# Gated cross-attention and quantised FFN on one core: input weights quantised in the drain, the first norm applied after the query projection, one-hots of batches 1 to 3 on GpSimd

## Chip, cores and metric

One core of one Trainium2 chip runs the whole layer. The metric is device time in microseconds of one execution. Engine names: PE (TensorE, with PEld for its weight loads), DVE (VectorE), ACT (ScalarE), POOL (GpSimd), SP (the queue that issues most loads).

## What is computed

x has 4 batches of 1024 rows of 256. Each row attends to 4 consecutive rows of a small context (77 rows), found by its segment number, with 16 heads of 16; then an FFN 256 to 1024 to 256 whose weights and activations are quantised.

```python
def reference(x, ctx_1024, itok_BxS_0_511, g_xattn, g_ffn, L0_xattn_Wq, L0_xattn_Wkv, L0_xattn_Wo, L0_ffn_W_in, L0_ffn_b_in, L0_ffn_W_out, L0_ffn_b_out):
    # _layernorm(x): (x - mean) / sqrt(var + 1e-5) over the last axis
    def _L0_xattn_ref(q, kv_src, seg_id, Wq, Wkv, Wo):      # 16 heads of 16, SCALE = 0.25
        qh = _split_heads(q @ Wq.T)
        k, v = jnp.split(kv_src @ Wkv.T, 2, axis=-1)
        kh, vh = _split_heads(k), _split_heads(v)
        gather = seg_id[:, :, None] - jnp.arange(4)
        neg_mask = gather < 0
        gc = jnp.clip(gather, 0, lkv - 1)
        k_sel, v_sel = kh[b_idx, :, gc], vh[b_idx, :, gc]
        scores = einsum('bhqd,bhqkd->bhqk', qh, k_sel) * SCALE
        probs = softmax(where(neg_mask, -inf, scores))
        return einsum('bhqk,bhqkd->bhqd', probs, v_sel).reshape(b, lq, 256) @ Wo.T
    def _L0_ffn_ref(x, W_in, b_in, W_out, b_out):
        # quantize_w8_per: round to 127 levels of the absolute maximum of a column (W_in) or a row (W_out)
        # quantize_a16: round to 32767 levels of the absolute maximum of the whole tensor
        hidden = gelu(quantize_a16(x) @ quantize_w8_per(W_in, 0) + b_in)
        return quantize_a16(hidden) @ quantize_w8_per(W_out, 1) + b_out
    x = x + tanh(g_xattn[0]) * _L0_xattn_ref(_layernorm(x), ctx_1024, itok_BxS_0_511, L0_xattn_Wq, L0_xattn_Wkv, L0_xattn_Wo)
    x = x + tanh(g_ffn[0]) * _L0_ffn_ref(_layernorm(x), L0_ffn_W_in, L0_ffn_b_in, L0_ffn_W_out, L0_ffn_b_out)
```

## The kernel before

The work is straight engine programs joined by semaphores. There are NT = 32 tiles of 128 rows, handled in NP = 16 pairs; TB = 8 tiles make a batch. The kernel has four parts.

**Setup.** Context and weights are transposed on PE. `project_kv(b)` makes K and V of a batch in PSUM, `kv_scales` and `kv_high`/`kv_low` split them into two f16 halves in `kvtab`. `clamp_seg(b)` (L903) clamps the segment numbers of a batch, broadcast over 80 partitions, and `make_onehot(b)` (L910) compares them with the partition number: four one-hot matrices of 80 x 1024, by which PE gathers K and V rows as matmuls. `neg` holds the mask of rows whose segment number is below the offset. The query weights are transposed into `wqT`.

**The attention steps.** `step(i)` exists on every engine and is a software pipeline over pairs: the first norm of pair i (`stats(0)`, `aggregate(0)`, `norm_bias`, `norm1`), transpose and query projection of pair i; products and scores of pair i-1 (`qk`, `qk_sum`, `mask`, `score_max`, `shift`); softmax and weighting of V of pair i-2 (`exp`, `exp_sum`, `probs`, `copy_v`, `weigh_v`); output projection and residual of pair i-3; second norm of pair i-4 (`stats(1)`, `aggregate(1)`, `norm2`); its transpose and maximum for pair i-5. Steps 1 to 5 and 16 to 20 are written out, 6 to 15 are a loop of two steps an iteration. Within a step DVE runs in the order: statistics, exp sum, aggregate (L796, it releases POOL), reciprocal, `probs` (L847), `qk` (L811), `norm_bias` (L803), sum (L817), `qk`, sum, `largest` (L860), `mask` (L823), `residual` (L854), `score_max`, `shift` (L832). POOL runs `inv_std` (L268, L270, the power -0.5) and then `weigh_v` for two tiles: L278 (products), L281 and L285 (sums). PE has one PSUM pair of banks for K (`ps_k`) and one for V (`ps_v`), so each gather waits until the tile before has been read.

**The weights of the FFN.** W_in is transposed into PSUM in two halves (`win_T`), scaled per row (`win_scales` on DVE), rounded to int16 and made f16 (`round_win` on ACT), transposed back (`win_back`) and kept as `win8`; this happens between steps 1 and 3. W_out is rounded on DVE in steps 19 and 20 (L989 to L1002), and its maximum over partitions is a GpSimd `partition_all_reduce` (L303).

**The FFN.** After step 20 (the drain) the maximum of the normed x over partitions (L307) gives the scale; stage B is `expand` on PE (L728), Gelu on ACT, `hidden_max` and `quantise_x` on DVE, 8 groups of 4 tiles; POOL adds the output bias to the residual (L313). After a last maximum (L316) stage C is `contract` (L757) with the rounding on ACT and DVE.

## Time and profile before

| | us |
|---|---|
| median of 3 runs | 381.46 (380.48 to 418.29) |
| the profiled execution, its own time | 379.69 |
| its span, first to last instruction | 377.9 |
| mean granted TensorE clock | 0.918 |
| DVE busy, share of the span | 313.8, 83% |
| PE busy, share of the span | 289.2, 77% |
| ACT busy, share of the span | 225.0, 60% |
| POOL busy, share of the span | 179.9, 48% |

The profiled execution lies 0.8 us below the fastest run. Its span leaves out 1.8 us that lie around it. Busy shares are means over parts with different limits: setup and first steps to about 77 us, attention steps to 220 us, the drain to 250.2 us, stage B to 308 us, stage C to 370 us.

### The profile page before, as it was taken

To read this page: it belongs to the slowest core of one execution; us is meant where nothing else is said; L and a number is where in the kernel's file an instruction comes from. 1 tells how busy PE (TensorE), PEld (TensorE's weight loads), DVE (VectorE), ACT (ScalarE), POOL (GpSimd) and SP (SyncE) were. 2 spreads that over 40 slices of the span, in tenths; PEclk is the share of its full clock that TensorE was granted. 3 is DMA by queue.
4 is the path that set the end of the run, shared out by engine and by line. 5 is a ranking of instruction groups with operands and counts; after the bars stand their busy time and mean duration, and the time that the engine had idled before them with its cause. 6 is when DMAs were issued, how large, how long until landed. Compare 5 with 4: busy or idle time off the path is not lost.

```text
span 377.9 us, 6301 instructions
## 1 busy us (share of the span) xinstructions
PE 289.2 (77%) x1801; PEld 209.9 (56%) x1801; DVE 313.8 (83%) x583; ACT 225.0 (60%) x343; POOL 179.9 (48%) x167
## 2 busy tenths in 40 slices
PE   0685766778887987889887755159999958999991
PEld 0452555556665866667666544014444427888881
DVE  0278779998999999999999963668999969999990
ACT  1145265526556456555555552319999969999981
POOL 0110076687887797877788892113324500110011
PEclk9998769969999899998999986559999998999997
DMA  7991000000000000000000000001121210345438
GB/s 254 283 393 36 3 0 0 3 0 0 3 1 0 0 0 0 0 2 0 0 0 0 0 0 0 1 3 56 78 88 56 99 69 0 57 62 91 69 56 113
DMA packets 7117, 17.71 MB, mean 47 GB/s; under 512 B 1334, under 2 KB 3838, under 8 KB 6590
## 3 DMA queue, kind: packets, MB, share of 16 engines
q1 hardware_dynamic: 4447, 12.57, 9.4%
q0 software_dynamic: 1296, 4.19, 7.4%
q10 hardware_dynamic: 1359, 0.76, 0.8%
q8 instruction: 8, 0.13, 0.1%
q14 instruction: 7, 0.06, 0.1%
HBM read 9.13 MB, written 8.39 MB: 46 GB/s over the span
## 4 chain that ended last, share of the span: by engine, by line
PE 43%; DVE 35%; issue 15%; POOL 3%; ACT 2%; DVEq 1%; POOLq 0%; ACTq 0%
PE bank L728 15%; PE bank L757 15%; DVE prod L811 9%; PE bank L608 6%; DVE s L817 5%; PE bank L588 3%; DVE bn L788 3%; DVE onehot L910 2%; DVE xres L854 2%; DVE nbias L803 1%; DVE mv L796 1%; PE bank L566 1%; POOL vsel L278 1%; DVE srec L841 1%; DVE s L823 1%
## 5 line engine op out<-in xcount | busy, mean ns | idle before, releaser
L588 PE MATMUL bank<-kvtab,onehot 80*128 (+1 forms) x512 | 71.4, 285 | 36.6 <-DVE prod L811 25.8
L588 PEld LDWEIGHTS bank<-kvtab,onehot 80*128 (+1 forms) x512 | 48.2, 101 | 56.9 <-issue 23.6
L278 POOL TENSOR_TENSOR vsel<-vsel,pr 128x1024 f32<-128x1024 f32 x32 | 61.7, 1930 | 0.0
L728 PE MATMUL bank<-xhi,win 128*128 128x512 f16 x128 | 49.7, 388 | 8.0 <-DVE xlo L1022 8.0
L487 ACT ACTIVATE hidden<-bank,bin__58,zscale 128x512 f32 x64 | 49.8, 778 | 8.0 <-PE bank L728 2.9
L728 PE MATMUL bank<-xlo,win 128*128 128x512 f16 x128 | 49.6, 387 | 0.0
L1074 DVE SCALAR_TENSOR_TENSOR hlo<-hq,rel_wout,hhi 128x512 f16<-128x512 int16 x64 | 45.7, 744 | 0.0
L1027 DVE TENSOR_REDUCE hmax<-hidden 128x1 f32<-128x1024 f32 (+1 forms) x32 | 38.0, 1215 | 8.9 <-ACT hidden L487 8.8
L757 PE MATMUL bank<-wout,hhi 128*128 128x256 f16 x256 | 39.3, 277 | 5.3 <-DVE hhi L1066 5.3
L281 POOL TENSOR_TENSOR vsel<-vsel 128x512 f32<-128x512 f32 x32 | 41.1, 1285 | 2.5
L811 DVE TENSOR_TENSOR prod<-bank,q 128x1024 f32<-128x1024 f32 x32 | 38.8, 1212 | 0.8 <-PE bank L588 0.8
L817 DVE TENSOR_REDUCE s<-prod 128x64 f32<-128x1024 f32 x32 | 38.8, 1213 | 0.6
L608 PE MATMUL bank<-woT,oT 128*128 128x256 f32 x128 | 38.5, 455 | 0.7 <-ACT oT L343 0.7
L757 PE MATMUL bank<-wout,hlo 128*128 128x256 f16 x256 | 39.0, 275 | 0.0
L268 POOL TENSOR_TENSOR ve<-mv,consts 128x4 f32<-128x4 f32 (+1 forms) x20 | 4.7, 233 | 69.4 <-DVE mv L796 69.4
L343 ACT ACTIVATE vsel<-bank 128x1024 f32<-128x1024 f32 x32 | 32.7, 1023 | 6.7 <-PE bank L588 5.7
L503 ACT ACTIVATE hq<-hidden,qh 128x1024 int16<-128x1024 f32 (+1 forms) x32 | 34.9, 1143 | 2.5 <-DVE qh L1055 2.5
L313 POOL TENSOR_TENSOR xres<-xres,bout 128x1024 f32<-128x1024 f32 x8 | 18.9, 2365 | 36.2 <-DVE xlo L1022 29.5
L379 ACT ACTIVATE xn<-xres,nbias,rstd 128x256 f32 (+1 forms) x32 | 17.5, 593 | 25.5 <-DVE nbias L803 25.5
L608 PE MATMUL bank<-wqT,xT 128*128 128x256 f32 x128 | 31.5, 390 | 1.1 <-ACT xT L343 1.1
L803 DVE SCALAR_TENSOR_TENSOR nbias<-mv,rstd 128x4 f32<-128x4 f32 (+1 forms) x20 | 26.8, 1338 | 6.2 <-POOL rstd L270 6.2
L608 PEld LDWEIGHTS bank<-woT,oT 128*128 128x128 f32 x128 | 28.0, 230 | 5.9 <-ACT oT L343 1.3
(113 smaller groups left out, 485.4 us busy)
## 6 DMA issues: line engine op xcount, KB each, us to landing
xres<-in_x_dram SPq DMA_DIRECT2D x4, 1024.0 KB, 18.1
out_dram<-xres SPq DMA_DIRECT2D x8, 512.0 KB, 2.6
out_dram<-y POOLq DMA_DIRECT2D x7, 512.0 KB, 5.3
win_ld<-in_L_ffn_W_in_dram SPq DMA_DIRECT2D x1, 1024.0 KB, 13.1
wout_ld<-in_L_ffn_W_out_dram SPq DMA_DIRECT2D x1, 1024.0 KB, 23.3
seg_i<-in_itok_BxS_dram SPq DMA_DIRECT2D x3, 320.0 KB, 14.3
wkv_ld<-in_L_xattn_Wkv_dram SPq DMA_DIRECT2D x1, 512.0 KB, 5.3
out_dram<-y POOLq DMA_DIRECT2D x2, 256.0 KB, 5.1
```

The costliest lines, as they stand in the source:

```text
L278: pool.tensor_tensor(v3, v3, pr[k][:, t].rearrange("p o h -> p (o h)").unsqueeze(2).broadcast_to([P, KW * H, HD]), ALU.mult).then_inc(s_pv, 1)
L281: pool.tensor_tensor(vsel[t][:, 0:2, :], vsel[t][:, 0:2, :], vsel[t][:, 2:4, :], ALU.add).then_inc(s_pv2, 1)
L487: act.activation(hidden[:, g, f, :], bank, ACT.Gelu, bias=bin_[:, f:f + 1], scale=zscale[:, f:f + 1]).then_inc(s_h, 1)
L503: act.activation(hq[m][:], hidden[:, g, 2 * m:2 * m + 2, :], ACT.Copy, scale=qh[:, 3:4]).then_inc(s_hq, 1)
L588: mm = pe.matmul(dst[:, off * D:(off + 1) * D], onehot[:, off, bass.ds(tile * P, P)], kvtab[:, b, part, col:col + D], start=(part == 0), s ...
L608: mm = pe.matmul(dst[:, t * D:(t + 1) * D], src[:, c, t * P:(t + 1) * P], w[:, c, :], start=(c == 0), stop=(c == C - 1))
L728: mm = pe.matmul(bank, win8[:, c, f * P:(f + 1) * P], part[k][:, c, :], start=(at == 0), stop=(at == 2 * C - 1))
L757: mm = pe.matmul(bank, part[f][:, t * P:(t + 1) * P], wout8[:, f, :], start=(f == 0 and r == 0), stop=(f == FC - 1 and r == 1))
L811: dve.tensor_tensor(prod[t][:], ps_k[:].rearrange("p (o d) -> p o d", o=KW), q[k][:, t, :].unsqueeze(1).broadcast_to([P, KW, D]), ALU.mult ...
L817: dve.tensor_reduce(s[k][:, t].rearrange("p o h -> p (o h)"), prod[t][:].rearrange("p o (h d) -> p (o h) d", h=H), AX.X, ALU.add).then_inc ...
L1027: dve.tensor_reduce(hmax[:, bass.ds(g * (FC // 2) + m, 1)], hidden[:, g, 2 * m:2 * m + 2, :], AX.XY, ALU.max, apply_absolute_value=True).t ...
L1074: dve.scalar_tensor_tensor(out=hlo[f][:], in0=hq[f // 2][:, f % 2, :], scalar=rel_wout[:, f:f + 1], in1=hhi[f][:], op0=ALU.mult, op1=ALU.s ...
```

## The change

1. **First norm past the query projection.** The mean over D is taken off the rows of the query weights (`centre_wq`), so that raw x can be transposed and projected; the reciprocal deviation is applied as a scale while q leaves PSUM (`evac_q`, now two activations). `norm1` and `xn` are gone. The statistics of x are taken a batch of 8 tiles at a time (`stats1`, with `inv_std1` on POOL): batch 0 in the setup, batches 1 to 3 at the start of steps 4, 5 and 6. `norm_bias` becomes two `tensor_scalar` on one column each.
2. **GpSimd clamps and makes the one-hots** of batches 1 to 3, ahead of all its steps; DVE makes those of batch 0.
3. **W_in is quantised in the drain**: `win_T` after step 17, `round_win(0)` and `win_back(0)` around steps 18 to 20, the second half after step 20. K and V of batches 2 and 3 are projected after step 1 in banks 6 and 7, where they were projected ahead of step 1 in banks 2 and 3.
4. **W_out is quantised in stage B**, before and after the maxima of the first group. The order of the two `partition_all_reduce` is exchanged, and one more stands ahead of POOL's first statistics.
5. **The last tile's V is weighted on DVE** (`weigh_last`), the one before on POOL.
6. The steps of the attention are written out on all engines; the loops over them are gone.

```diff
+            def inv_std1(b):
+
+                at = slice(b * TB, (b + 1) * TB)
+                pool.wait_ge(s_mv1, b + 1)
+                pool.tensor_tensor(ve1[:, at], mv1[:, at, 1], consts[:, 0:TB], ALU.add).then_inc(s_ve1, 1)
+                pool.wait_ge(s_ve1, b + 1)
+                pool.tensor_tensor(rstd1[:, at], ve1[:, at], consts[:, TB:2 * TB], ALU.pow).then_inc(s_rstd1, 1)
...
-                    weigh_v(i - 2, k, 1)
+                    if i < NP + 1:
+                        weigh_v(i - 2, k, 1)
 
             pool.wait_ge(s_const, 2)
-            for i in range(6):
+            pool.partition_all_reduce(qx[:, 7:8], consts[:, 0:1], P, RMAX).then_inc(s_lib, 1)
+            inv_std1(0)
+
+            def make_onehot(b):
+
+                pool.wait_ge(s_segb[b], 16)
+                pool.tensor_scalar(seg_b[:, b * LQ:(b + 1) * LQ].rearrange("u (t p) -> u t p", t=TB),
+                                   seg_i[:, b * LQ:(b + 1) * LQ].rearrange("u (p t) -> u t p", t=TB),
+                                   float(U - 1), 0.0, ALU.min, ALU.max).then_inc(s_segc, 1)
+                pool.wait_ge(s_segc, b)
+                pool.wait_ge(s_kvscale, b // 2 + 1)
+                for off in range(KW):
+                    ins = pool.tensor_scalar(onehot[:, off, b * LQ:(b + 1) * LQ], seg_b[:, b * LQ:(b + 1) * LQ],
+                                             jo[:, off:off + 1], kvp[:, 3, b:b + 1], ALU.is_equal, ALU.mult)
+                ins.then_inc(s_ohp, 1)
+
+            for b in range(1, NB):
+                make_onehot(b)
+            for i in range(NP + 4):
+                if 4 <= i <= NB + 2:
+                    inv_std1(i - 3)
                 step(i, i % 2)
-            with pool.Fori(3, NP // 2) as j:
-                for k in range(2):
-                    step(2 * j + k, k)
-            for i in range(NP, NP + 4):
-                step(i, i % 2)
+
+            pool.wait_ge(s_xall, 1)
+            pool.partition_all_reduce(qx[:, 1:2], qx[:, 0:1], P, RMAX).then_inc(s_qxr, 1)
...
-                copy(q[k][:].rearrange("p t d -> p (t d)"), ps_q).then_inc(s_q, 1)
+                act.wait_ge(s_rstd1, u // (TB // 2) + 1)
+                for t in range(2):
+                    ins = act.activation(q[k][:, t, :], ps_q[:, t * D:(t + 1) * D], ACT.Copy,
+                                         scale=rstd1[:, 2 * u + t:2 * u + t + 1])
+                ins.then_inc(s_q, 1)
...
-            round_win(0)
+            step(1, 1)
             kv_high(2)
             kv_high(3)
-            step(1, 1)
+            for i in range(2, NP + 3):
+                step(i, i % 2)
+            round_win(0)
+            step(NP + 3, 1)
+            keep_win8(0)
+            step(NP + 4, 0)
             round_win(1)
...
+            keep_win8(1)
...
-            weight_T(ps_o, wq_ld, s_wq, s_wqTp)
...
+            weight_T(ps_o, wq_ld, s_wqc, 1, s_wqTp)
...
             queries(0, 0)
-            pe.wait_ge(s_win, 16)
-            pe.wait_ge(s_woT, 1)
-            win_T(0)
             pe.wait_ge(s_oh, 1)
             pe.wait_ge(s_kvlo, 2)
             gather_k(0, 0)
+            step(1, 1)
+            pe.wait_ge(s_woT, 1)
             project_kv(2)
             project_kv(3)
-            step(1, 1)
-            pe.wait_ge(s_winq, 2)
+            step(2, 0)
+            pe.wait_ge(s_kvlo, NB)
+            for i in range(3, NP + 2):
+                if 4 <= i <= NB + 1:
+                    pe.wait_ge(s_ohp, i - 3)
+                step(i, i % 2)
+            pe.wait_ge(s_win, 16)
+            pe.wait_ge(s_prod, 2 * NP)
+            win_T(0)
+            pe.wait_ge(s_lastpv, 1)
             win_T(1)
-            pe.wait_ge(s_kvlo, NB)
...
+            step(NP + 2, 0)
+            step(NP + 3, 1)
+            pe.wait_ge(s_oT, NP)
+            win_back(0)
+            step(NP + 4, 0)
+            pe.wait_ge(s_x1, NP)
+            win_back(1)
...
+            def stats1(b):
+                dve.wait_ge(s_x[b], 16)
+                if b:
+                    dve.wait_ge(s_mv1, b)
+                for t in range(TB):
+                    ins = dve.bn_stats(bn1[:, t, :], xres[:, b * TB + t, :])
+                ins.then_inc(s_bn1, 1)
+                dve.wait_ge(s_bn1, b + 1)
+                for t in range(TB):
+                    ins = dve.bn_aggr(mv1[:, b * TB + t, :], bn1[:, t, :])
+                ins.then_inc(s_mv1, 1)
...
-                dve.scalar_tensor_tensor(out=nbias[k][:, at], in0=mv[k][:, at, 0], scalar=-1.0, in1=rstd[k][:, at],
-                                         op0=ALU.mult, op1=ALU.mult).then_inc(s_nb, 1)
+                    ins = dve.bn_aggr(mv[k][:, t, :], bn2[k][:, t, :])
+                ins.then_inc(s_mv, 1)
+
+            def norm_bias(u, k):
+                dve.wait_ge(s_rstd, u + 1)
+                if u >= 2:
+                    dve.wait_ge(s_xn2, u - 1)
+                for t in range(2):
+                    ins = dve.tensor_scalar(nbias[k][:, t:t + 1], mv[k][:, t, 0:1], rstd[k][:, t:t + 1], -1.0, ALU.mult, ALU.mult)
+                ins.then_inc(s_nb, 1)
+
+            def centre_wq():
+                dve.wait_ge(s_wq, 16)
+                link(dve.tensor_reduce(wq_mean[:], wq_ld[:], AX.X, ALU.add))
+                link(dve.tensor_scalar(wq_mean[:], wq_mean[:], -1.0 / D, None, ALU.mult))
+                for c in range(C):
+                    ins = dve.tensor_scalar(wq_ld[:, c, :], wq_ld[:, c, :], wq_mean[:, c:c + 1], None, ALU.add)
+                ins.then_inc(s_wqc, 1)
...
+            def weigh_last(u, k):
+
+                dve.wait_ge(s_vp, 2 * NP)
+                dve.wait_ge(s_p, NP)
+                dve.tensor_tensor(prod[1][:].rearrange("p o (h d) -> p (o h) d", h=H), ps_v[:].rearrange("p (n d) -> p n d", d=HD),
+                                  pr[k][:, 1].rearrange("p o h -> p (o h)").unsqueeze(2).broadcast_to([P, KW * H, HD]),
+                                  ALU.mult).then_inc(s_lastpv, 1)
+                dve.wait_ge(s_lastpv, 1)
+                dve.wait_ge(s_oTp, u - 1)
+                dve.tensor_reduce(o[k][:, 1, :], prod[1][:].rearrange("p o d -> p d o"), AX.X, ALU.add).then_inc(s_olast, 1)
...
-            dve.wait_ge(s_x[0], 16)
-            stats(0, 0, 0)
-            aggregate(0, 0, 0, 0)
+            centre_wq()
             dve.wait_ge(s_jo, 1)
             clamp_seg(0)
-            norm_bias(0, 0)
-
+            stats1(0)
+
+            kv_scales(0)
+            make_onehot(0)
+            kv_low(0)
+            kv_low(1)
             dve.wait_ge(s_segt, 16)
             link(dve.tensor_scalar(seg_f[:], seg_t[:], 0.0, None, ALU.max))
             for off in range(KW):
                 ins = dve.tensor_scalar(neg[:, :, off], seg_f[:], float(off), NEG, ALU.is_lt, ALU.mult)
             ins.then_inc(s_neg, 1)
-            kv_scales(0)
-            make_onehot(0)
-            kv_low(0)
-            kv_low(1)
-            clamp_seg(1)
-            make_onehot(1)
-            win_scales(0)
             dve.wait_ge(s_neg, 1)
+            step(1, 1)
             kv_scales(2)
-            step(1, 1)
+            step(2, 0)
             kv_low(2)
             kv_low(3)
-            win_scales(1)
-            step(2, 0)
-            clamp_seg(2)
-            make_onehot(2)
             dve.wait_ge(s_tanh, 1)
             step(3, 1)
-            for b in range(3, NB):
-                clamp_seg(b)
-                make_onehot(b)
-            for b in range(1, NB):
-                dve.wait_ge(s_x[b], 16)
-            for i in range(4, 6):
+            for i in range(4, NP + 2):
+                if i <= NB + 2:
+                    stats1(i - 3)
                 step(i, i % 2)
-            with dve.Fori(3, NP // 2) as j:
-                for k in range(2):
-                    step(2 * j + k, k)
-            for i in range(NP, NP + 3):
-                step(i, i % 2)
-
+            win_scales(0)
+            step(NP + 2, 0)
+            step(NP + 3, 1)
+            win_scales(1)
+            step(NP + 4, 0)
...
+            quantise_x(1, 1)
             dve.wait_ge(s_wout, 16)
             link(dve.tensor_reduce(amax_wout[:], wout_ld[:], AX.X, ALU.max, apply_absolute_value=True))
             link(dve.tensor_scalar(amax_wout[:], amax_wout[:], AMAX_FLOOR, None, ALU.max))
             dve.tensor_reduce(top_wout[:, 0:1], amax_wout[:], AX.X, ALU.max).then_inc(s_wrow, 1)
             link(dve.reciprocal(sc_wout[:], amax_wout[:]))
             link(dve.tensor_scalar(sc_wout[:], sc_wout[:], W_LEVELS, None, ALU.mult))
-            step(NP + 3, 1)
+            stage_b(0, 0)
```

## Rows read from the trace of the kernel before

**Rows 1.** The page, part 4: the chain that ended last, by engine.

```profile
PE 43%; DVE 35%; issue 15%; POOL 3%; ACT 2%; DVEq 1%; POOLq 0%; ACTq 0%
```

**Rows 2.** Timeline, step 16: start us, us, engine, line, operation, tiles.

```profile
209.04 0.23 DVE L796 BATCH_NORM_AGGREGATE mv<-bn 128x2 f32<-128x6 f32 x2
...
209.63 0.78 POOL L270 TENSOR_TENSOR rstd<-ve,consts 128x2 f32<-128x2 f32 x1
...
210.38 1.93 POOL L278 TENSOR_TENSOR vsel<-vsel,pr 128x1024 f32<-128x1024 f32 x1
...
210.89 1.43 DVE L803 SCALAR_TENSOR_TENSOR nbias<-mv,rstd 128x2 f32<-128x2 f32 x1
...
214.42 1.93 POOL L278 TENSOR_TENSOR vsel<-vsel,pr 128x1024 f32<-128x1024 f32 x1
...
216.35 0.28 DVE L823 TENSOR_TENSOR s<-s,neg 128x128 f32<-128x128 f32 x1
...
218.76 0.23 DVE L796 BATCH_NORM_AGGREGATE mv<-bn 128x2 f32<-128x6 f32 x2
```

**Rows 3.** Timeline of the start, up to the first steps.

```profile
23.70 1.91 DVE L910 TENSOR_SCALAR onehot<-seg_b,jo,kvp 80x1024 bf16<-80x1024 bf16 x4
...
27.94 3.60 PE L566 MATMUL bank<-wkvT,ctxT 128*80 128x512 f32 x8
...
34.65 1.19 DVE L811 TENSOR_TENSOR prod<-bank,q 128x1024 f32<-128x1024 f32 x1
...
40.85 2.69 PE L608 MATMUL bank<-wqT,xT 128*128 128x256 f32 x8
...
50.83 1.92 POOL L278 TENSOR_TENSOR vsel<-vsel,pr 128x1024 f32<-128x1024 f32 x1
...
58.21 1.08 DVE L903 TENSOR_SCALAR seg_b<-seg_i 80x1024 bf16<-80x1024 int32 x1
58.22 1.67 POOL L285 TENSOR_TENSOR o<-vsel 128x256 f32<-128x256 f32 x1
```

**Rows 4.** Timeline of step 4.

```profile
74.35 1.39 DVE L788 BATCH_NORM_STATS2 bn<-xres 128x6 f32<-128x256 f32 x4
...
77.71 1.93 POOL L278 TENSOR_TENSOR vsel<-vsel,pr 128x1024 f32<-128x1024 f32 x1
```

**Rows 5.** Groups by line and form, GpSimd: busy us, mean ns, idle before.

```profile
L281 POOL TENSOR_TENSOR vsel<-vsel 128x512 f32<-128x512 f32 x32 | 41.1, 1285 | 2.5
...
L257 POOL TENSOR_SCALAR_AFFINE_SELECT ident<-ident 128x128 f16<-128x128 f16 x1 | 0.3, 283 | 0.0
...
L251 POOL MEMSET ident<- 128x128 f32 x1 | 0.2, 204 | 0.3 <-POOLq L1099 0.3
...
L260 POOL IOTA jo<- 80x4 f32 x1 | 0.1, 137 | 0.0
```

**Rows 6.** Timeline of the drain, to the first FFN matmuls.

```profile
228.26 1.12 PE L579 MATMUL bank<-ident,o 128*128 128x128 f32 x4 [4.08 <-POOL o L285]
...
234.50 2.28 DVE L989 TENSOR_REDUCE amax_wout<-wout_ld 128x8 f32<-128x2048 f32 x1
...
239.65 0.16 DVE L803 SCALAR_TENSOR_TENSOR nbias<-mv,rstd 128x2 f32<-128x2 f32 x1 [1.08 <-POOL rstd L270]
...
245.36 0.38 POOL L303 PARTITION_ALL_REDUCE top_wout<-top_wout  x1 [5.75 <-issue]
...
247.35 0.37 POOL L307 PARTITION_ALL_REDUCE qx<-qx  x1 [1.60 <-DVE qx L1007]
...
250.22 0.58 PE L728 MATMUL bank<-xhi,win 128*128 128x512 f16 x1 [8.04 <-DVE xlo L1022]
...
254.41 2.35 POOL L313 TENSOR_TENSOR xres<-xres,bout 128x1024 f32<-128x1024 f32 x1 [6.70 <-issue]
```

**Rows 7.** Stretches: length, PE, PEld, DVE, ACT, POOL busy (x), PEclk, DMA, GB/s.

```profile
220.00:250.20 30.20, 10.58 (x35) 7.58 (x33) 17.00 (x43) 7.99 (x13) 10.39 (x13) 0.61 0.00 1
250.20:308.00 57.80, 57.31 (x256) 25.41 (x256) 48.93 (x53) 49.52 (x65) 18.86 (x8) 0.97 0.18 73
```

More of the change, by code:

```diff
@@ L371, in round_win, with norm2 @@
                 copy(win_f16[:, fs, :], w_i16[:, fs, :]).then_inc(s_winq, 1)
[L373 to L383 removed]
+            def norm2(u, k):
                 if first(u, 2):
```

214 lines of the change are left out of this document (91 added, 123 removed).

## The prediction, made before the changed kernel was run

> **What bounds the kernel now.** I read the chain of waits first: PE and DVE share it, and nearly all of the PE part is the FFN [rows 1], which the change leaves alone. So the question is the 250 us ahead of stage B. There I read the timeline of one step that is already written out and already without the first statistics, step 16 [rows 2]. The reader is to see two clocks in it. DVE goes from one aggregate to the next in 218.76 - 209.04 = 9.72 us. POOL goes aggregate, power, two weighings 4.04 us apart, and is done some 0.5 us ahead of the next aggregate. And DVE loses time to POOL in one place: nbias (L803) takes 1.43 us, ending where POOL's first L278 ends (210.38 + 1.93 = 212.31), while the same instruction takes 0.16 us when POOL is idle [rows 6]. A DVE instruction with two inputs in SBUF waits out the POOL instruction that is running. It goes the other way too, and the two alternate: L285 took 1.67 us behind a DVE clamp of 1.08 us [rows 3].
>
> **The steps.** From the weighing at 77.71 (step 4) [rows 4] to the one at 210.38 (step 16) [rows 2] lie 132.7 us, 11.06 a step. Afterwards such a step has no first statistics, no loop branch and a power over two columns, which is just what step 16 is now: 9.72 us. The shorter nbias gains nothing beside it, as far as I can see: all of DVE comes 1.0 us earlier, and then the mask (L823, two SBUF inputs, now at 216.35) is ready at 215.35, in the middle of POOL's second L278 (214.42 to 216.35), and waits that 1.0 us. What nbias no longer waits for, the mask will. The moved statistics come back in steps 4 to 6: four bn_stats take 1.39 us [rows 4], eight with eight aggregates (0.23 us for two [rows 2]) 3.4 us, and POOL's add and power over eight columns stand ahead of the pair's own, which I put at 0.9 us more on the path (two columns take 0.78 us [rows 2], eight are not in the trace: between 0.78 and four times that I take 1.8 us, half of it hidden behind the second statistics). So two of the twelve steps take 9.72 + 4.3 = 14.0 us and ten 9.72: 125.2 us, a gain of **7.5 us**.
>
> **The one-hots on GpSimd.** The trace has no tensor_scalar on POOL. The nearest rows for one instruction of 1024 columns [rows 5]: the fill at (204 - 137) / 124 = 0.5 ns a column from the iota up (0.7 us for 1024), the affine select at (283 - 137) / 124 = 1.18 ns (1.34 us), and the two-input L281 at 1285 / 512 = 2.5 ns (2.6 us). I take the affine select, since it also reads, compares and selects, and 1.7 us for the clamp, which reads every eighth element; both ends are kept for the range.
> [...]
>
> **The start.** kv_scales ends at 23.70 now, where the one-hots begin [rows 3]. Centring the weights adds 1.7 us and eight tiles of statistics 2.4 us, the mask and norm bias come off: 25.6. POOL is not free earlier: with the new partition reduce it changes its library twice, 5.75 us there and 6.70 us back [rows 6], from 12.7 to 25.5. From then on DVE's small SBUF instructions and POOL's alternate: the four one-hots of batch 0 (1.91 us now [rows 3]) with add, power, clamp and one-hot, then the five for the mask (L953, L955) with one-hots and the second clamp. Going through it turn by turn, the first product begins at 39.5, for 34.65 now [rows 3]. K and V of batches 2 and 3 are projected only behind step 1's gathers and queries on PE: the queries end 8.9 us behind the first product, the projection takes 3.60 [rows 3], the scales 2.0: 54.0. There POOL stands waiting, and only then makes one-hots of batch 2, clamps and makes those of batch 3: 8 x 1.42 + 1.8, with 1.0 for DVE's turns, to 68.2. All that is queued on POOL behind it is the weighing of pair 0, which begins at 50.83 now [rows 3]. **Loss 17.4 us**, whatever DVE saves by not making 12 one-hots and 3 clamps.
> From there to the weighing of step 4 it takes 77.71 - 50.83 = 26.9 us now. Afterwards: two weighings 8.2; the PE was blocked at the transpose of o, so transpose, two gathers and the second product 5.2, sum, mask, residual and shift 4.0, eight statistics 3.4, the rest to the power 2.2, the power of eight 0.9: 23.9. Gain **3.0 us**, no one-hots lying between.
>
> **The drain.** Now: the last o is transposed at 228.26, the residual is done at 234.5, DVE then takes 3.0 us for W_out ahead of the last statistics, nbias is at 239.65, POOL's library change takes 5.75 us, the maxima follow, and the first FFN matmul is at 250.22 [rows 6]. Afterwards DVE weighs the last tile, and o is ready 4.0 us earlier. But PE has 16 transposes of W_in and one of xn2 ahead of it, at a mean clock of 0.61 [rows 7] and four transposes in 1.12 us [rows 6]: 4.3 to 5.5 us if the clock stays low, about half if it rises. I count 1.2 us gained of the 4.0. The W_out work leaves: 2.8 us. The library change stays (the early one is undone by the way back to the ordinary library), begins right behind the last power at 239.6 and now hides the last maxima, W_in's second scales included: first matmul 239.6 + 5.75 + (250.22 - 247.35) = 248.2, 2.0 us earlier. Second half of W_in: ACT needs it 8 us behind nbias, in time for the fifth chunk. Sum **6.0 us** gained.
>
> **Stage B** takes W_out, 6.1 us of DVE. DVE is busy 48.9 of 57.8 us there [rows 7] and the last two groups have no quantising, so it should be absorbed; 0 to 2 us, I take 0. If it were not, PE would wait for xlo of group 3.
> ACT loses norm1 and stays below DVE; the raw transposes free PE of a wait.
>
> **Sum.** 379.69 + 17.4 - 3.0 - 7.5 - 6.0 + 0 = 380.6 for the profiled execution; its own time is 1.8 us below the median of the runs. I predict **380 us**, between the two readings (the profile's difference is +0.9, that to the median -1.5): no change that can be measured.
>
> **Rivals.**
> (a) POOL's one-hots are cheap and the alternation is kinder than I assume. A microsecond less in a one-hot is 12 us less in the total (8 behind the second scales, some 4 in the turns at the start). At 0.95 us, between fill and affine select, that is 4.8 us, and DVE keeping its turn over its mask instructions 3 more: 373. At the fill's 0.7 us and the same, 370. For it: the fill's row. Against it: every other POOL row of this size is over 1.2 us. Chance 0.30. A mask that finds a gap instead of L278 gives 1.0 us more for each of 12 steps and belongs here.
> (b) POOL's one-hots run like its two-input instructions. At L281's slope, (1285 - 137) / 508 = 2.26 ns or 2.45 us each, 1.1 us more at 12 to one are 13 us: 394. Place: the weighing of pair 0. From 2.0 us a one-hot it is over 2% slower. Chance 0.19.
> (c) The two small tensor_scalar of nbias each wait for a POOL instruction, the second losing its turn to L281: 1.3 us in each of 12 steps, 396. The trace has no single-column tensor_scalar beside a busy POOL; bounds 0.3 us and 2.8 us a step. [...] Chance 0.07.
> (d) As forecast: 0.44.
>
> **Range.** 368 (a, its far end) to 394 (b). The likeliest case's own range is 374 to 387. Faster by over 2% needs 373.8: 0.30. Slower by over 2%, over 389: 0.24. Within: 0.46; 2% is about what a measurement of this kernel tells from no change.
>
> **What would show it.** First product near 39.5 and first weighing (L278's successor) near 68; POOL tensor_scalar at 1.3 us; DVE small instructions of up to 1.5 us at 26 to 40; steps 7 to 16 at 9.7 us with the mask ending where the second weighing product ends; three steps of 14 us; a POOL gap of 5.75 us ahead of the reduce in the drain; stage B as long as before. Wrong if: the first weighing is near 55, which would be some 12 us of gain; steps at 9.0; or nbias still at 1.5 us.

## The result, and the profile after

The changed kernel takes 399.28 us (median of 4 runs, 396.55 to 400.17) against 381.71 us for the kernel before in the same comparison: a ratio of 1.046, with an interval of 1.039 to 1.053. One run of the kernel before, of 418.29 us, was in a slower state that the chip has, and the ratio leaves it out. The changed kernel is slower, and it lies outside the predicted range. The profiled execution takes 400.14 us with a span of 398.3 us (before: 379.69 and 377.9).

I read the chain of waits of the changed kernel first, by engine and then by line.

```profile
DVE 36%; PE 34%; POOL 18%; issue 7%; ACT 3%; POOLq 0%; ACTq 0%; DVEq 0%
PE bank L779 14%; PE bank L750 12%; POOL onehot L323 11%; DVE prod L856 7%; DVE s L862 5%; DVE s L868 3%; PE bank L609 3%; DVE bn L813 3%; DVE xres L910 2%; PE bank L629 2%; POOL vsel L293 2%; DVE hmax L1051 2%; DVE xmax L916 2%; DVE bn L823 2%; POOL seg_b L317 1%
```

POOL held 3% of this chain before [rows 1] and holds 18% now; the one-hots alone are 11% of the span. Before, no one-hot was made on POOL. The timeline of POOL at the start shows them all:

```profile
19.27 0.87 POOL L311 PARTITION_ALL_REDUCE qx<-consts  x1 [6.45 <-issue]
27.40 0.28 POOL L273 TENSOR_TENSOR ve<-mv,consts 128x8 f32<-128x8 f32 x1 [7.27 <-issue]
...
29.45 2.03 POOL L317 TENSOR_SCALAR seg_b<-seg_i 80x1024 bf16<-80x1024 int32 x1
31.59 15.11 POOL L323 TENSOR_SCALAR onehot<-seg_b,jo,kvp 80x1024 bf16<-80x1024 bf16 x4
46.66 2.03 POOL L317 TENSOR_SCALAR seg_b<-seg_i 80x1024 bf16<-80x1024 int32 x1
48.79 15.07 POOL L323 TENSOR_SCALAR onehot<-seg_b,jo,kvp 80x1024 bf16<-80x1024 bf16 x4
63.83 2.01 POOL L317 TENSOR_SCALAR seg_b<-seg_i 80x1024 bf16<-80x1024 int32 x1
65.94 15.06 POOL L323 TENSOR_SCALAR onehot<-seg_b,jo,kvp 80x1024 bf16<-80x1024 bf16 x4
80.97 1.93 POOL L293 TENSOR_TENSOR vsel<-vsel,pr 128x1024 f32<-128x1024 f32 x1
```

Four one-hots take 15.1 us, so one takes 3.78 us. From 29.45 to 80.97 us POOL has hardly a gap, and the line at its end is the first weighing (L293 is L278 of before), which stood at 50.83 [rows 3]. On VectorE the four one-hots of batch 0, the first product and the first mask and subtraction are these:

```profile
25.70 1.91 DVE L962 TENSOR_SCALAR onehot<-seg_b,jo,kvp 80x1024 bf16<-80x1024 bf16 x4
...
30.57 1.22 DVE L856 TENSOR_TENSOR prod<-bank,q 128x1024 f32<-128x1024 f32 x1 [1.07 <-ACT q L449]
...
35.65 1.07 DVE L868 TENSOR_TENSOR s<-s,neg 128x128 f32<-128x128 f32 x1
...
37.16 0.29 DVE L877 TENSOR_TENSOR s<-s,smax 128x128 f32<-128x128 f32 x1
```

DVE makes the same four in 1.91 us, eight times as fast. Its first product stands at 30.57, which is 4.1 us earlier than before and 9 us earlier than forecast. The last two lines lie beside POOL's second one-hot (35.4 to 39.2): the mask, with two inputs in SBUF, waits 0.8 us for it, and the subtraction, of the same kind and begun in its middle, does not wait. So it is with all of them: in this kernel and in experiments 3 and 8, seven masks, subtractions and probabilities that began within 1.0 us of the start of a one-hot were held until 1.04 us behind it, and seven that began later took their usual 0.29 us. A one-hot of 3.78 us holds VectorE for its first 1.0 us only.

The groups by line and form of the changed kernel (busy us, mean ns of one, idle before) show the bias and the mask:

```profile
L868 DVE TENSOR_TENSOR s<-s,neg 128x128 f32<-128x128 f32 x16 | 18.6, 1165 | 0.1
L840 DVE TENSOR_SCALAR nbias<-mv,rstd 128x1 f32<-128x1 f32 x32 | 5.2, 205 | 3.5 <-POOL rstd L285 3.5
```

A bias of one column takes 0.2 us though POOL is busy beside it (two in turn 0.33 us, where one instruction took 1.43 [rows 2]). The mask took 0.28 us in the step of [rows 2]; now its mean is 1.17.

Two stretches of the changed kernel by engine (the columns are those of [rows 7]), first the block of one-hots, then the drain from the last pairs' weighing to the first FFN matmul:

```profile
29.50:81.00 51.50, 23.70 (x94) 15.31 (x92) 21.51 (x30) 7.39 (x15) 51.20 (x17) 0.63 0.01 2
```

```profile
230.80:262.50 31.70, 18.35 (x107) 14.49 (x106) 24.76 (x57) 16.92 (x31) 14.87 (x17) 0.77 0.00 1
```

In the first, POOL is busy for 51.2 of 51.5 us and DVE for 21.5. And in stage B the quantising of group 2 and the W_out work run into POOL's additions of the output bias (L344). The last line of DVE is the low half of group 3:

```profile
274.50 2.94 DVE L1042 TENSOR_SCALAR xr<-xn2T,qx 128x1024 int16<-128x1024 f32 x1
...
278.54 4.28 DVE L1073 TENSOR_SCALAR w_i<-wout_ld,sc_wout 128x256 int16<-128x256 f32 x8
...
289.80 0.69 DVE L1046 TENSOR_TENSOR xlo<-xr,xhi 128x1024 f16<-128x1024 int16 x1
```

```profile
274.54 2.35 POOL L344 TENSOR_TENSOR xres<-xres,bout 128x1024 f32<-128x1024 f32 x1 [6.92 <-issue]
278.71 2.39 POOL L344 TENSOR_TENSOR xres<-xres,bout 128x1024 f32<-128x1024 f32 x1 [1.82 <-DVE xlo L1046]
```

Between the two, in a stretch that before was all TensorE, PE has 2.15 us of work in 6.60 and then waits for that xlo. The first matmul behind the wait is of 0.60 us, where the last one ahead of it took 0.38, and the stretch after it has a lower granted clock:

```profile
284.00:290.60 6.60, 2.15 (x10) 0.78 (x8) 6.50 (x9) 2.88 (x4) 0.03 (x1) 0.85 0.00 0
290.60:300.00 9.40, 9.38 (x33) 3.80 (x34) 8.81 (x10) 5.24 (x7) 4.68 (x2) 0.74 0.14 56
```

```profile
290.62 0.60 PE L750 MATMUL bank<-xhi,win 128*128 128x512 f16 x1 [4.47 <-DVE xlo L1046]
```

Laid against the kernel before, with the first FFN matmul now at 262.49 and the last all-reduce at 330.30 (310.12 before):

| from, to | before | predicted | after | predicted change | measured change |
|---|---|---|---|---|---|
| start, first weighing | 50.83 | 68.2 | 80.97 | +17.4 | +30.1 |
| first weighing, weighing of step 4 | 26.88 | 23.9 | 23.73 | -3.0 | -3.2 |
| to the weighing of step 16 | 132.7 | 125.2 | 126.1 | -7.5 | -6.6 |
| to the first FFN matmul | 39.8 | 33.8 | 31.7 | -6.0 | -8.1 |
| stage B, to its last all-reduce | 59.9 | 59.9 | 67.8 | 0 | +7.9 |
| the rest | 67.8 | 67.8 | 68.0 | 0 | +0.2 |

So the three gains came about as forecast, and two terms of the sum did not: the start and stage B.

### The profile page after: what moved, and what is told of

It reads as the page before. It is cut to its first block, busy times and chain, and to the rows that moved or that the text cites. A ratio compares the mean times of both kernels' runs of the same rounds, so it can differ in the third digit from the quotient of the medians.

```text
span 398.3 us, 5777 instructions
## 1 busy us (share of the span) xinstructions
PE 302.2 (76%) x1801; PEld 217.9 (55%) x1801; DVE 306.7 (77%) x586; ACT 209.7 (53%) x327; POOL 224.9 (56%) x180
## 4 chain that ended last, share of the span: by engine, by line
DVE 36%; PE 34%; POOL 18%; issue 7%; ACT 3%; POOLq 0%; ACTq 0%; DVEq 0%
PE bank L779 14%; PE bank L750 12%; POOL onehot L323 11%; DVE prod L856 7%; DVE s L862 5%; DVE s L868 3%; PE bank L609 3%; DVE bn L813 3%; DVE xres L910 2%; PE bank L629 2%; POOL vsel L293 2%; DVE hmax L1051 2%; DVE xmax L916 2%; DVE bn L823 2%; POOL seg_b L317 1%
## 5 line engine op out<-in xcount | busy, mean ns | idle before, releaser
L609 PE MATMUL bank<-kvtab,onehot 80*128 80x256 f16 x512 | 76.8, 300 | 19.3 <-DVE prod L856 12.3
L609 PEld LDWEIGHTS bank<-kvtab,onehot 80*128 80x128 bf16 x512 | 52.2, 107 | 39.4 <-DVE prod L856 17.4
L293 POOL TENSOR_TENSOR vsel<-vsel,pr 128x1024 f32<-128x1024 f32 x31 | 59.9, 1931 | 0.0
L750 PE MATMUL bank<-xhi,win 128*128 128x512 f16 x128 | 51.7, 404 | 5.8 <-DVE xlo L1046 4.5
L750 PE MATMUL bank<-xlo,win 128*128 128x512 f16 x128 | 51.5, 402 | 0.0
L323 POOL TENSOR_SCALAR onehot<-seg_b,jo,kvp 80x1024 bf16<-80x1024 bf16 x12 | 45.2, 3781 | 0.3
L344 POOL TENSOR_TENSOR xres<-xres,bout 128x1024 f32<-128x1024 f32 x8 | 18.9, 2363 | 36.5 <-DVE xlo L1046 29.6
L600 PE MATMUL bank<-ident,o 128*128 128x128 f32 x64 | 11.1, 301 | 35.4 <-POOL o L300 35.4
L374 ACT ACTIVATE xT<-bank 128x512 f32<-128x512 f32 x16 | 9.6, 597 | 53.9 <-PE bank L659 53.9
L354 POOL DMA_DIRECT2D out_dram<-y x7 | 6.3, 906 | 51.3 <-ACT y L539 51.3
L629 PE MATMUL bank<-wqT,xT 128*128 128x256 f32 x128 | 34.5, 417 | 0.4 <-ACT xT L374 0.4
## 6 DMA issues: line engine op xcount, KB each, us to landing
seg_i<-in_itok_BxS_dram SPq DMA_DIRECT2D x3, 320.0 KB, 15.1
```

Of the source, the lines that this page charges most:

```text
L293: pool.tensor_tensor(v3, v3, pr[k][:, t].rearrange("p o h -> p (o h)").unsqueeze(2).broadcast_to([P, KW * H, HD]), ALU.mult).then_inc(s_pv, 1)
L323: ins = pool.tensor_scalar(onehot[:, off, b * LQ:(b + 1) * LQ], seg_b[:, b * LQ:(b + 1) * LQ], jo[:, off:off + 1], kvp[:, 3, b:b + 1], ALU ...
L374: return act.activation(dst, src, ACT.Copy)
L609: mm = pe.matmul(dst[:, off * D:(off + 1) * D], onehot[:, off, bass.ds(tile * P, P)], kvtab[:, b, part, col:col + D], start=(part == 0), s ...
L629: mm = pe.matmul(dst[:, t * D:(t + 1) * D], src[:, c, t * P:(t + 1) * P], w[:, c, :], start=(c == 0), stop=(c == C - 1))
L750: mm = pe.matmul(bank, win8[:, c, f * P:(f + 1) * P], part[k][:, c, :], start=(at == 0), stop=(at == 2 * C - 1))
```

## The experiments

The kernel before took 381.63 us (median) beside the first four experiments, 381.16 beside the next four and 380.8 beside the last three. A kernel's profiled run is one execution; where kernels are compared by place, that place is the start of the named instruction.

**1. The one-hots back on VectorE.** Clamp and one-hots of batches 1 to 3 go between DVE's steps, and all else stays as changed.

```diff
-            for b in range(1, NB):       # GpSimd
-                make_onehot(b)
             step(1, 1)                   # VectorE
+            clamp_seg(1)
+            make_onehot(1)
             kv_scales(2)
...
             kv_low(3)
+            clamp_seg(2)
+            make_onehot(2)
             dve.wait_ge(s_tanh, 1)
             step(3, 1)
+            clamp_seg(3)
+            make_onehot(3)
```

> The changed kernel with clamps and one-hots of batches 1 to 3 back on DVE (batch 1 between step 1 and the second scales, where DVE stood idle 5.7 us; batch 2 behind step 2, batch 3 behind step 3). Theory A, POOL's 12 one-hots of 3.78 us and 3 clamps of 2.03 us are the whole loss at the start: the first weighing comes near 48 (81.0 in the changed kernel), that of step 4 near 80 (104.7), and the time is 24 us below the changed kernel's, 375 to 377. Rival B, the start is held by something else (the library changes, K and V of batches 2 and 3 projected late, slow TensorE clock): the first weighing stays above 60 and the time above 385. Rival C, the low clock (0.86) costs time by itself and returns with PE busy: then also the steps 4 to 6 get shorter than 13.7 us.

Measured: 372.33 us, ratio to before 0.978 (0.973 to 0.983). The whole change but for this one part is 2.2% faster than the kernel before (1.7 to 2.7%). The first weighing stands at 49.27, and one batch costs DVE 3.0 us where it cost POOL 17.2:

```profile
38.02 1.09 DVE L953 TENSOR_SCALAR seg_b<-seg_i 80x1024 bf16<-80x1024 int32 x1
39.14 1.91 DVE L960 TENSOR_SCALAR onehot<-seg_b,jo,kvp 80x1024 bf16<-80x1024 bf16 x4
```

**2. W_out's work moved within stage B.** From the changed kernel, the reduction goes ahead of the wait for the partition maximum, and the rounding goes by twos behind the maxima of the last group but one.

```diff
+            link(dve.tensor_reduce(amax_wout[:], wout_ld[:], ...))
             dve.wait_ge(s_qxr, 1)
...
+            for m in range(FC // 2):
+                hidden_max(NG - 2, m)
+                for f in (2 * m, 2 * m + 1):
+                    ins = dve.tensor_scalar(w_i16[:, f, :], wout_ld[:, f, :], sc_wout[:, f:f + 1], ...)
```

> The changed kernel with only the W_out work moved inside the FFN's first half: its maximum where DVE waits for the partition reduce in the drain, its rounding two pieces behind each maximum of the last but one group, the rest in the last group. Theory A, stage B lost 7.9 us (59.9 to 67.8, first FFN matmul to the last partition reduce) because DVE was late with xlo of group 3 and PE stood still from 284 to 290.6 and lost its clock: stage B goes back to 60 to 62 us and the time falls by 6 to 8 us. Rival B, it is only the slow start of PE's clock (half speed to 268.0): stage B stays at 66 or more. [...]

Measured: 396.49 us, ratio 1.041 (1.038 to 1.044), 2.8 us below the changed kernel by the medians and not the 6 to 8 expected. Its stage B took 64.0 us for 67.8. TensorE no longer stops for group 3, but the work now lies where nothing follows that could take it up, and the first two roundings meet L344 there: they take 3.90 us together, the next two 0.60. That is 3.3 of the 4.1 us by which the stage is still longer than before: half of the loss stays, where theory A had it gone and rival B had a stage of 66 us or more. PE has nothing left in the last 4.5 us of the stage while DVE is still at it:

```profile
308.00:318.00 10.00, 7.95 (x37) 3.43 (x35) 9.97 (x13) 8.07 (x11) 3.26 (x2) 1.00 0.26 106
318.00:322.50 4.50, 0.00 (x0) 0.00 (x0) 4.29 (x8) 0.00 (x0) 0.00 (x0) 0.80 0.01 2
```

**3. One batch on GpSimd, two on VectorE.** As in experiment 1, but POOL makes batch 1.

> The changed kernel with GpSimd making the one-hots of batch 1 alone, DVE those of batches 2 and 3. POOL is free from 29.5 us and its first weighing can't begin before 47, which is 17.5 us, and a batch takes 17.2 us. Theory A: it fits just about, first weighing at 47 to 49, and the time equals that of the kernel with all on DVE within 1 us, since the 3 us saved on DVE were taken from its idle time. Rival B, DVE's small instructions wait for POOL's long ones (up to 3.8 us each at mask, shift and probabilities): 2 to 5 us slower than with all on DVE.

Measured: 372.28 us, 0.974 (0.969 to 0.979), the same as experiment 1. Its first weighing is at 48.08. One batch (17.2 us) fits into the time in which POOL would wait for the first probabilities anyway (19.05 us in experiment 1); three (51.5 us) do not.

**4. What a GpSimd tensor_scalar costs.** Experiment 1 with nine probes on POOL ahead of its first weighing, their results unused.

> The kernel with all one-hots on DVE, and nine GpSimd tensor_scalar of 80 x 1024 on scratch tiles ahead of POOL's steps, each alone: the one-hot's form (equal to a column's value, times a column's value), the same with two multiplications, with constants in place of the columns, equality alone, one multiplication alone, then the one-hot's form, equality alone and a multiplication alone in f32, and the clamp on contiguous int32. Only their durations are read. Theory A, the compare is the price: both forms with equality near 3.8 us, those without near 1 to 2 us, whatever the type. Theory B, bf16 is the price (conversion both ways): f32 forms under 2 us. Theory C, the two operands per partition are the price: constants bring it under 2 us. [...]

Measured (one run, 375.85 us, each probe once); the timeline of the probes, the columns start us, us:

```profile
29.56 3.80 POOL L334 TENSOR_SCALAR scr_h<-seg_b,jo,kvp 80x1024 bf16<-80x1024 bf16 x1
33.46 1.20 POOL L336 TENSOR_SCALAR scr_h<-seg_b,jo,kvp 80x1024 bf16<-80x1024 bf16 x1
34.74 4.53 POOL L338 TENSOR_SCALAR scr_h<-seg_b 80x1024 bf16<-80x1024 bf16 x1
39.36 2.82 POOL L340 TENSOR_SCALAR scr_h<-seg_b 80x1024 bf16<-80x1024 bf16 x1
42.26 2.82 POOL L342 TENSOR_SCALAR scr_h<-seg_b 80x1024 bf16<-80x1024 bf16 x1
45.19 3.79 POOL L344 TENSOR_SCALAR scr_f<-xres,jo,kvp 80x1024 f32<-80x1024 f32 x1
49.08 2.95 POOL L346 TENSOR_SCALAR scr_f<-xres,jo 80x1024 f32<-80x1024 f32 x1
52.12 2.77 POOL L348 TENSOR_SCALAR scr_f<-xres 80x1024 f32<-80x1024 f32 x1
54.98 1.04 POOL L350 TENSOR_SCALAR scr_h<-seg_i 80x1024 bf16<-80x1024 int32 x1
```

In this order they are: compare and multiply by two columns of scalars (the one-hot); two multiplications by the same columns; compare and multiply by constants; the comparison alone; one multiplication by a constant alone; the one-hot in f32; the comparison with a column alone in f32; one multiplication by a constant alone in f32; the clamp of unbroken elements. The element type is not the price (3.80 and 3.79), and the scalars' columns are not (constants take 4.53). Two multiplications take 1.20, but one alone takes 2.82, as much as one comparison. So the forms differ by a factor of nearly four, and the number of operations does not order them. What makes a form cheap stays open: the two multiplications and the single one differ in their scalars too, columns against a constant. The clamp takes 1.04 us without the stride of eight and 2.03 with it.

**5. W_out's work in two gaps of VectorE.** From experiment 1: the reduction lies under POOL's all-reduce, the rounding and the cast lie between the second quantised group and the first hidden maximum.

```diff
             dve.tensor_scalar(bout[:], bout[:], tanhs[:, 1:2], None, ALU.mult)
+            link(dve.tensor_reduce(amax_wout[:], wout_ld[:], ...))
+            ... floor, row maximum, reciprocal, scale
             dve.wait_ge(s_qxr, 1)
...
             quantise_x(1, 1)
+            dve.wait_ge(s_winq, 4)
+            for f in range(FC):
+                ins = dve.tensor_scalar(w_i16[:, f, :], wout_ld[:, f, :], sc_wout[:, f:f + 1], ...)
+            link(ins)
+            dve.tensor_copy(wout8[:], w_i16[:])
             stage_b(0, 0)
-            the same roundings and cast
```

> The changed kernel with its one-hots on VectorE as in the first experiment, and the W_out work of VectorE in two stretches where that run shows it idle: the reduction behind 'largest x' while GpSimd reduces over the partitions (VectorE stood 2.58 us at 230.6), the eight roundings and the cast between the second quantised group and the first hidden maximum. Reference for both theories: 372.3 us for the first experiment, its stage B 65.65 us against 59.9 before. Theory A (stage B lost its 5.7 us because VectorE, 92% busy in its steady part, had no room for the W_out work and TensorE stood for the third group's low half): stage B back to 60 to 61 us, time 366 to 368 us. Rival B (the loss is the slow clock at stage B's start, which has nothing to do with W_out): stage B stays at 64 or more, time 371 to 373 us.

Measured: 365.94 us, ratio 0.961 (0.957 to 0.964). Theory A holds. (The edit also brings W_out's all-reduce forward, to 232.20, and with it POOL's additions; what that is worth by itself was not tried.) Stage B goes from 234.88 to 295.84, 61.0 us, although it too begins on the lower clock (a mean of 0.61 of full in the 10 us from 233). In the nine kernels that keep W_out's work where the change put it (the changed one and experiments 1, 3, 4, 6, 7, 8, 10 and 11) it takes 65.6 to 67.9, and in each of them PE stops for group 3, for 4.1 to 4.5 us; here it does not. DVE's timeline here:

```profile
229.39 2.28 DVE L1038 TENSOR_REDUCE amax_wout<-wout_ld 128x8 f32<-128x2048 f32 x1
...
236.87 2.19 DVE L1077 TENSOR_SCALAR w_i<-wout_ld,sc_wout 128x256 int16<-128x256 f32 x8
...
249.09 2.35 DVE L1083 TENSOR_SCALAR rel_wout<-amax_wout,top_wout 128x8 f32<-128x8 f32 x1
```

The reduction begins where DVE had nothing to do, and the roundings take 2.19 us instead of 4.28. The third line is a new thing to see: an operation of eight columns takes 2.35 us, because POOL's addition runs from 249.06 for 2.35 us.

**6. The norm bias in one instruction again.** Experiment 1 with `scalar_tensor_tensor` over two columns in place of the two `tensor_scalar`.

> The first experiment with the norm bias of both tiles in one scalar_tensor_tensor of two columns again, as before the change. Theory A (in the steps after the fourth the wait for GpSimd's weighing is only handed from the bias to the mask, so that splitting the bias gained nothing of itself): steps stay at 9.7 us, the bias takes 1.2 to 1.5 us in them and the mask 0.3, time within 1.5 us of 372.3 us. Rival B (the split bias is what made the steps shorter): about 0.9 us more in each of 12 steps, 381 to 384 us.

Measured: 373.45 us, 0.980 (0.977 to 0.982), 1.1 us above experiment 1 by the medians, with intervals that overlap. The steps from the seventh pair on are 9.78 us apart, against 9.68. The groups of this kernel:

```profile
L837 DVE SCALAR_TENSOR_TENSOR nbias<-mv,rstd 128x2 f32<-128x2 f32 x16 | 22.2, 1389 | 3.4 <-POOL rstd L285 3.4
L865 DVE TENSOR_TENSOR s<-s,neg 128x128 f32<-128x128 f32 x16 | 5.9, 369 | 0.1
```

One of the two waits for GpSimd: the bias here (1.39 us, mask 0.37), the mask in the changed kernel (1.17 us, bias 2 x 0.2). The edit moves the wait and is worth 0.1 us a step.

**7. Without the all-reduce at GpSimd's start.** Experiment 1 less that one instruction.

> The first experiment without the all-reduce at the start of GpSimd. Theory A (that instruction loads nothing that lasts: the reduction ahead of the feed-forward part waits 5.9 us for its library all the same, and at the start GpSimd comes back from it only at 27.9 us although its means were ready at 23.6): rstd ready some 4 us earlier, the first product 0.5 to 1.1 us earlier (VectorE is busy till 30.2 us), the idle time ahead of the reduction unchanged at 5.9 us, time 371 to 372.3 us. Rival B (it does warm the library): the idle time ahead of that reduction grows by some us and the time by 1 to 4 us.

Measured: 370.9 us, 0.972 (0.967 to 0.976). POOL's add comes at 23.17 and not at 27.9, the first product at 30.69 for 31.29. Ahead of the real reduction POOL stands at least as long as in experiment 1 (5.94 us):

```profile
232.63 0.38 POOL L332 PARTITION_ALL_REDUCE qx<-qx  x1 [6.33 <-issue]
```

In experiment 5, with the early reduce, that wait is 5.79 us, in experiment 9, without it, 5.86. So that instruction does not shorten it by anything that shows, and rival B is out. (That a change of library fills this time is my reading; the traces show that POOL stands, not why.) Whether taking it away gains the 1.4 us of the medians stays open: the intervals of this run and of experiment 1 overlap.

**8. One one-hot a step.** The changed kernel with batch 1 on DVE, and on POOL one instruction behind the weighings of each of the steps 2 to 9.

```diff
                 step(i, i % 2)
+                if 2 <= i <= 5:
+                    one(2, i - 2)
+                if 6 <= i <= 9:
+                    one(3, i - 6)
```

> The changed kernel with batch 1's one-hots on VectorE and those of batches 2 and 3 on GpSimd one instruction a step, in steps 2 to 9, where each is 3.8 us beside weighings of 6.4 us in a step of 9.7. Theory A (price times place: GpSimd has 3.3 us free in a step, so 0.5 us a step too little, and VectorE's operations that wait for it wait longer): 374 to 379 us. Rival B (only the block ahead of the first weighing cost anything, spread they are free): 371 to 373 us. Rival C (each holds VectorE off for its whole 3.8 us): 390 us or more.

Measured: 383.5 us, ratio 1.007 (1.004 to 1.009): 11 us over experiment 1, more than theory A's 2 to 7 and less than rival C. My expectation had counted 6.4 us of weighing in a step and left out o's addition (0.73 us a tile). A tile takes 4.05 us, the pair with its add and power 9.2, so POOL had 0.5 us free in a step of 9.68 and not 3.3. A plain step with a one-hot takes 12.83 us, 3.15 more for an instruction of 3.8; the first eight steps together take 107.7 us for 97.6 in experiment 1. One stretch of such steps:

```profile
117.00:142.70 25.70, 20.96 (x121) 16.51 (x121) 20.67 (x36) 11.27 (x20) 24.92 (x19) 0.87 0.00 1
```

POOL 24.9 of 25.7 us: it is the bound there. VectorE is busy for 20.7 us of it, and a one-hot holds it for 1.0 us only.

**9. All that helped.** Experiment 5 with experiment 7's edit, and with the three small operations on W_out's ratio ahead of the roundings.

> The fifth kernel (one-hots on VectorE, W_out work in the two gaps) without the all-reduce at GpSimd's start, and with the three small operations on W_out's row ratio moved from behind group 0 to ahead of the eight roundings, since the one of 8 columns took 2.35 us beside GpSimd's addition of the output bias (2.35 us, from the same instant). Theory A (both changes take away waits that lay on the path): 1.4 us from the first, as the seventh kernel measured it against the first experiment, and 0.5 to 1.5 us from the second: 363.5 to 365 us. Rival B (TensorE bounds stage B by now, so only the first counts, or neither does): 365 to 366 us.

Measured: 365.31 us, ratio 0.958 (0.955 to 0.960), the fastest of all and 8.5% faster than the changed kernel; against experiment 5 it is no measurable difference, as rival B had it. Stage B again takes 61.0 us. The ratio's operation is back to 0.23 us, but then the cast comes at 239.53 and meets POOL's addition of 239.41:

```profile
239.53 2.76 DVE L1082 CAST wout<-w_i 128x2048 f16<-128x2048 int16 x1
```

It took 0.69 us in experiment 5. The wait is gone from the ratio and has come at the cast, one of 2.1 us for another.

**10. The last tile's weighing on GpSimd.** Experiment 1 with `weigh_last` undone.

> The first experiment (372.3 us) with the last tile's weighing back on GpSimd, and its values copied by ScalarE, as before the change. Theory A (the last tile's output is on the path of the drain: VectorE has it 1.21 + 1.94 us after it can begin, beside GpSimd's own tile, where GpSimd would do both in turn, 3.9 us each): 2 to 3.5 us slower, 374.3 to 375.8 us. Rival B (VectorE's 3.15 us are on the path just as much): within 1 us.

Measured: 374.65 us, 0.981 (0.978 to 0.984): 2.3 us more than experiment 1, as theory A has it, with runs that overlap (372.79 to 374.86 and 370.81 to 374.06). In the trace o is whole 8.1 us behind the start of the last pair's weighing (215.12), since POOL does the tiles in turn; in experiment 1 it is 4.1. The last line of it here:

```profile
222.52 0.72 POOL L300 TENSOR_TENSOR o<-vsel 128x256 f32<-128x256 f32 x1
```

Of those 4.0 us, 2.1 arrive at the first FFN matmul (32.8 us behind the weighing of step 16 for 30.7), and kernels with the same drain as experiment 1 scatter by 1.5 there (experiment 6 took 32.2). That o is whole 4.0 us earlier is shown; what of it reaches the time is not.

**11. The changed kernel at the price that was forecast.** Twelve instructions of POOL multiply where they should compare, so the tables are not one-hots and the result is wrong, and everything else is the changed kernel's.

```diff
-                                             jo[:, off:off + 1], kvp[:, 3, b:b + 1], ALU.is_equal, ALU.mult)
+                                             jo[:, off:off + 1], kvp[:, 3, b:b + 1], ALU.mult, ALU.mult)
```

> The changed kernel as it is, but GpSimd's twelve instructions multiply where they should compare, so that the tables they select by hold products and not one-hots: everything else, places, waits and sizes, is as in the changed kernel. The probe had this form at 1.20 us against 3.80. Theory A (only the price was wrong: GpSimd is through 3 x 2.03 + 12 x 1.20 = 20.5 us after 29.5, at 50.0, and VectorE goes on beside it): the first weighing at 50 to 51 us, the time 30 us below the changed kernel's, 367 to 372 us. Rival B (the prediction's turns between VectorE and GpSimd come back at its price of 1.34 us): first weighing at 60 to 68, time 378 to 386 us.

Measured: 372.49 us, 0.983 (0.978 to 0.988), 27 us below the changed kernel. The timeline of POOL:

```profile
31.48 4.72 POOL L323 TENSOR_SCALAR onehot<-seg_b,jo,kvp 80x1024 bf16<-80x1024 bf16 x4
36.18 2.03 POOL L317 TENSOR_SCALAR seg_b<-seg_i 80x1024 bf16<-80x1024 int32 x1
45.04 4.75 POOL L323 TENSOR_SCALAR onehot<-seg_b,jo,kvp 80x1024 bf16<-80x1024 bf16 x4 [6.83 <-DVE kvp L976]
...
51.90 4.78 POOL L323 TENSOR_SCALAR onehot<-seg_b,jo,kvp 80x1024 bf16<-80x1024 bf16 x4
```

At 1.2 us an instruction POOL does stand waiting for the second scales, as the prediction said; my expectation of 50 us for the first weighing had forgotten that wait. It came at 56.7, the forecast's chain had it at 68.2. Yet the time is experiment 1's: from the first weighing to the one of step 4 it takes 23.6 us here and 29.8 there, where DVE makes two batches in between.

## Why the prediction was wrong

**The price of a one-hot: the step that failed.** "I take the affine select": 1.34 us, in the term of the start. It was 3.78 us, above the far end of the bounds too (2.6 us, and 2.45 in rival b). The nearest rows were other instructions of the engine, and none of them bounds this form: experiment 4 finds 1.20 to 4.53 us for tensor_scalar of one and the same size. Experiment 11 gives the size of the error: the same kernel at 1.2 us an instruction is 26.8 us faster, 2.2 us for each of twelve. Rival (b) had the direction, the place (the weighing of pair 0) and the point ("over 2% slower" from 2.0 us a one-hot), and its price was too low as well. Nor does a one-hot run like a two-input instruction: L278, with two inputs and all of 1024 columns, takes 1.93 us [rows 2], half of a one-hot and less than the 2.45 that the rival drew from L281. That row of the right size lay there unused.

No run shows the 0.95 us of rival (a) either. The cheapest forms run were the unbroken clamp (1.04) and two multiplications (1.20), and the kernel's own form is three times the latter. The clamp, put at 1.7 us, took 2.03 with its stride.

**How many lie on the path.** The forecast had 8 of 12 behind the second scales. With POOL busy from 29.45 without a gap, all twelve and the three clamps count (12 x 3.78 + 3 x 2.03 = 51.5 us, the length of the block); the second scales were ready while POOL was still at batch 1.

**The turns between DVE and POOL at the start.** Forecast: first product at 39.5. Measured: 30.57. POOL came to its add, 7.27 us behind the early all-reduce, only at 27.40, when DVE's one-hots were nearly over (27.6), and the five small ones for the mask ran without a wait. So no such turns took place in the start, and behind a one-hot a turn would have been of 1.0 us and not of its whole length. Experiment 11 separates this error from the price: at about the price that I assumed (1.19 us), the first weighing comes 11.5 us earlier than I had it, 9 of them because the second scales are ready at 45.0 and not at 54.0, and the kernel is at 372.5, where my sum says 380. Two errors of opposite sign stood in the term of +17.4; the price was the larger. Even a right price would not have given a right number by my chain.

**Stage B: 0 forecast, +7.9 measured.** The prediction had the right alternative in one sentence ("PE would wait for xlo of group 3") and gave it no weight. Two stretches of stage B in the kernel before, which I had not looked at apart:

```profile
250.20:260.00 9.80, 9.78 (x37) 4.09 (x38) 5.64 (x7) 6.26 (x9) 2.35 (x1) 0.80 0.14 55
...
270.00:280.00 10.00, 10.00 (x48) 4.54 (x47) 9.32 (x11) 9.07 (x12) 4.74 (x2) 1.00 0.13 52
```

DVE is busy for 5.64 of 9.8 us at the beginning, and for 9.3 of 10 after that. So the idle time that I counted, 8.9 of 57.8 us [rows 7], lay to nearly half (4.2 us) in the first 9.8 us; another 1.7 lay in the last 8. In the changed kernel only W_out's reduction lies at the beginning; the roundings come in the full part and push group 3 back, and the work meets POOL's additions, which make an instruction twice to four times as long (2.94 for 0.75 us, 4.28 for 2.19). PE then waits 4.5 us for group 3, and the wait costs again behind it: at a granted clock of 0.74 in the next 9.4 us I estimate 2.4 us more, and 0.9 for the start of the stage (0.70 in the first 9.5 us for 0.80 in 9.8). Together that is 7.8 of the 7.9 us. Experiment 5 takes 4.7 us out of the stage by the place of this work (6.8 against the changed kernel's). The 1.1 us that are left to the 59.9 of before would fit the lower clock at the beginning (0.70 in its first 9.8 us here, 0.80 before); that was not tried by itself.

**What held.** The steps: 9.68 us against 9.72 forecast, those with statistics 13.7 for 14.0, and one more of 11.6 us, 1.9 over a plain one; less what the others came in under, that is the 0.9 us by which the sum was off. (The prediction puts eight statistics and eight aggregates at 3.4 us; its own rows add up to 3.7, and the trace has 2.71 and 0.65.) The mask takes over the bias's wait, which experiment 6 shows by undoing it. The stretch from first weighing to step 4: -3.2 for -3.0. Rival (c) is out: single-column instructions took 0.2 us beside a busy POOL. The drain: -8.1 for -6.0; POOL's wait of 5.86 us ahead of the all-reduce stands in it as forecast (5.75), and the early all-reduce does not shorten it (experiment 7); no run shows that it is a change of library, as the forecast calls it; what the last tile on DVE is worth, 1.2 in my sum, experiment 10 does not settle. PE's transposes of W_in, which I had priced at the clock of before, lie in a stretch of 0.77 of full and not 0.61.

## What to carry to other kernels

Before work goes to GpSimd, price its exact form, operation by operation: forms of one instruction of one size differ here by a factor of four (1.20 to 4.53 us), and no neighbour's row bounds them. Then count what the engine has free in one step, every instruction of it included, since a block ahead of the first consumer costs all of its length that the engine would not have waited (31.7 of 51.5 us here, against experiment 1). Idle time of an engine is a place and not a sum: work moved into a stage must go where the gap is (under a reduction, ahead of the first result), and away from GpSimd's two-input instructions (a scaling of 0.75 us took 2.94 beside one); where a wait is removed, look at what then meets it.
